# A three-layer graph network on one core: dense tiles and some edge results kept in SBUF between stages, and a row of zeros for each partition

## What is computed

```
h  = relu(layernorm(x))
xn = bn(h, g0, be0)
h  = bn(relu(gcn_conv(xn, src, dst, ew, W1, b1)), g1, be1)                 # 128 -> 256
h  = bn(relu(graph_conv(h, src, dst, ew, Wrel2, brel2, Wroot2)), g2, be2)  # 256 -> 256
h  = bn(relu(graph_conv(h, src, dst, ew, Wrel3, brel3, Wroot3)), g3, be3)  # 256 -> 128
out = x + h

graph_conv(x): agg = segment_sum(ew * x[src], dst);  agg @ Wrel + brel + x @ Wroot
gcn_conv(x):   xw = x @ W; deg = segment_sum(ew, dst) + 1; norm = deg[src]^-.5 * ew * deg[dst]^-.5
               segment_sum(norm * xw[src], dst) + xw / deg + b
bn(x, g, b):   g * (x - mean) * rsqrt(var + eps) + b      (mean and var over the 100,000 nodes)
```

## Time and profile before

| | us |
|---|---|
| median of 3 runs | 3562.28 |
| lowest, highest | 3558.31, 3564.93 |
| profiled execution | 3567.39 |
| its span | 3565.6 |
| TensorE busy | 2930.0 (82%) |
| VectorE busy | 2611.3 (73%) |
| ScalarE busy | 2320.7 (65%) |
| DMA | 1142 MB, 320 GB/s over the span |

### The profile page before, as it was taken

One profiled execution on the slowest core, in us unless ns is written; L12 is line 12 of the kernel. 1 busy time (PEld: TensorE's weight loads), 2 busy tenths in 40 slices (PEclk: granted clock), 3 DMA queues, 4 the chain that ended last, 5 costly groups with the idle time before them and its releaser, 6 DMA issues. The chain is left out here.

```text
span 3565.6 us, 52119 instructions
## 1 busy us (share of the span) xinstructions
PE 2930.0 (82%) x12445; PEld 1951.0 (55%) x12445; DVE 2611.3 (73%) x5600; ACT 2320.7 (65%) x4070; POOL 1332.1 (37%) x1194
## 2 busy tenths in 40 slices
PE   3666599999996799999999999699999999554543
PEld 3665355555553567677777777455555555433432
DVE  6997488888887688888888888568777778433332
ACT  4999377777764677778787778456666666333332
POOL 1657555555551222222222220122223220266476
PEclk9999799999998899999999999899999999555555
DMA  5998499999996899999999999699999999899998
GB/s 200 346 345 301 153 331 333 332 331 333 333 331 240 266 347 341 336 336 341 340 338 342 340 338 313 207 290 344 346 346 351 346 343 321 324 367 364 382 357 238
DMA packets 344636, 1142.09 MB, mean 320 GB/s; under 512 B 55625, under 2 KB 103266, under 8 KB 294386
## 3 DMA queue, kind: packets, MB, share of 16 engines
q1 hardware_dynamic: 221468, 933.98, 69.5%
q0 software_dynamic: 62656, 77.70, 13.5%
q10 hardware_dynamic: 60438, 129.60, 10.2%
HBM read 625.81 MB, written 515.28 MB: 320 GB/s over the span
## 5 line engine op out<-in xcount | busy, mean ns | idle before, releaser
L1210 POOL DMA_INDIRECT l_ed_gathered<-agg_rows,pos_cols x392 | 432.5, 1103 | 1455.0 <-PE l_ps L1222 692.6
L1118 DVE TENSOR_TENSOR l_dn_hi<-l_dn_hi,l_dn_top 128x512 fp32r<-128x512 f32 x784 | 501.1, 688 | 234.5 <-ACT l_dn_top L1086 234.2
L1059 PE MATMUL l_ps<-l_dn_top,wroot_top 128*128 128x512 f32 x1176 | 503.8, 428 | 80.7 <-ACT l_dn_ho L1073 44.2
L1073 ACT ACTIVATE l_dn_ho<-l_ps,bias_fold 128x512 f32<-128x512 f32 x588 | 394.5, 681 | 156.2 <-PE l_ps L1059 155.3
L1086 ACT ACTIVATE l_dn_top<-l_dn_hi 128x512 fp32r<-128x512 f32 x784 | 447.5, 622 | 45.5 <-DMA l_dn_hi<-h_dense 45.5
L1059 PE MATMUL l_ps<-l_dn_hi,wroot_top 128*128 128x512 f32 x1176 | 466.8, 397 | 0.0
L1059 PE MATMUL l_ps<-l_dn_top,wroot_rest 128*128 128x512 f32 x1176 | 466.0, 396 | 0.0
L1648 POOL DMA_INDIRECT out<-out_rows_dst,out_cols x196 | 305.0, 1556 | 282.9 <-DMA out<-out_od_ot 182.7
L716 PE MATMUL l_ps<-l_dn_columns,w_fold 128*128 128x512 f32 x784 | 381.2, 609 | 30.5 <-ACT l_dn_ho L751 30.5
L1107 DVE BATCH_NORM_STATS2 bn_stats_all<-l_dn_ho 128x512 f32 (+1 forms) x588 | 365.7, 679 | 2.4 <-ACT l_dn_ho L1073 2.0
L1669 PE MATMUL out_ps<-ident,out_od_hi 128*128 128x128 f32 x784 | 192.8, 427 | 178.9 <-ACT out_od_hi L1657 178.9
(11 more groups left out here) (237 smaller groups left out, 5797.5 us busy)
## 6 DMA issues: line engine op xcount, KB each, us to landing
h_dense<-l_dn_ho SPq DMA_DIRECT2D x196, 1024.0 KB, 10.8
l_dn_hi<-h_dense SPq DMA_DIRECT2D x196, 1024.0 KB, 10.4
l_dn_rows<-h_rows SPq DMA_DIRECT2D x98, 520.0 KB, 6.4
h_rows<-norm_ln_ho SPq DMA_DIRECT2D x97, 520.0 KB, 4.2
h_dst<-l_ed_ho SPq DMA_DIRECT2D x98, 512.0 KB, 10.3
l_ed_hd<-h_dst ACTq DMA_DIRECT2D x98, 512.0 KB
h_dense<-l_dn_ho SPq DMA_DIRECT2D x98, 512.0 KB, 11.6
out_od_hi<-h_dense SPq DMA_DIRECT2D x98, 512.0 KB, 15.1
```

The source lines that it names most:

```text
L1059: ins = pe.matmul(o, a, b, start=t == 0, stop=t == len(terms) - 1)
L1073: act.activation(ho[:, j, m, c * CW:(c + 1) * CW], ps[:, u % 2, 0:CW], ACT.Relu, bias=bf[:, m:m + 1]).then_inc(rl[j], 1)
L1118: dve.tensor_tensor(rest[:, j, k, cc], hi[:, j, k, cc], top[:, j % 2, k, cc].bitcast(FP), ALU.subtract).then_inc(spl[j], 1)
L1210: pool.indirect_dma_start(tg[:, j, g, :], None, tab[n - 1][:, :], bass.IndirectOffsetOnAxis(ap=pos_c[:, t:t + 1], axis=0)).then_inc(gat[j] ...
```

## The change

It has four parts.

1. The last four dense tiles of l1 are copied from `dn_ho` into a buffer `hi_keep` that lives through l1, l2 and l3, and not stored to DRAM; l2 takes them as its first four tiles. l2 does the same for l3. l3 writes all its results into `ho_keep`, stores all but the last four, and out begins with these. A tile held in a slot keeps it, so the order of the tiles turns by four each time: l1 starts at tile 12 and ends with 8 to 11, so that out has the natural order. The reads of `h0` in l1 follow a list, so l1's last four rounds, not one, are written out (`tail`).
2. In l3 the destination results of even chunks (25 of 49) go to `rows_even` in SBUF, and out reads them there.
3. The first four tiles of x are loaded at the end of l3, where the stores of its last four tiles were.
4. `pos` of a node without incoming edge is EP + p on partition p, so 128 rows of zeros are read and not one. The rows were there already.

```diff
+def order_of(slots, total, moves):
+    order = list(range(total))
+    for _ in range(moves):
+        last = order[:slots]
+        order = order[slots:] + [last[p % slots] for p in range(total - slots, total)]
+    return order
...
+        hi_keep = sb("dense_tiles", [C, NS, 2, W])
...
+                pool.iota(own_zero_row[:, :], pattern=[[0, 1]], base=EP, channel_multiplier=1).then_inc(cst, 1)
...
+                link(dve.tensor_copy(no_edge_row[:, 0, :], own_zero_row[:, :]))
...
-                dve.memset(ho[:, :, :, C:C + 1], float(EP)).then_inc(preset, 1)
+                dve.tensor_copy(ho.rearrange("p s g c -> p (s g) c")[:, :, C:C + 1], no_edge_row.broadcast_to([P, LS * G, 1])).then_inc(preset, 1)
...
+            order = order_of(NS, NT, 3)
             def sync(sp):
                 def load(i, j):
+                    k = i * NS + j
                     wait_use(sp, tu[j], i - 1, CH)
-                    sp.dma_start(ht[:, j, :, :], tile_of(h0, i * NS + j, NP)).then_inc(got[j], 16)
+                    sp.dma_start(ht[:, j, :, :], tile_of(h0, order[k] if isinstance(i, int) else k + 3 * NS, NP)).then_inc(got[j], 16)
                 def store(i, j):
                     wait_use(sp, rl[j], i, per)
-                    sp.dma_start(h1[i * NS + j], ho[:, j, :, :]).then_inc(sto[j], 16)
+                    if isinstance(i, int) and i * NS + j >= NT - NS:
+                        sp.dma_start(hi_keep[:, j, :, :], ho[:, j, :, :]).then_inc(kept[j], 16)
+                    else:
+                        sp.dma_start(h1[i * NS + j], ho[:, j, :, :]).then_inc(sto[j], 16)
...
-            hi = ph.sb("dn_hi", [C, NS, kb, W])
+            hi, kept = hi_keep, ph.slots("dn_kept", NS)
+            def loaded(eng, i, j):
+                if not isinstance(i, int) or i > 0:
+                    wait_use(eng, got[j], i - 1, 16)
             def sync(sp):
                 def load(i, j):
-                    wait_use(sp, mm[j], i - 1, per)
-                    k = i * NS + j
-                    sp.dma_start(hi[:, j, :, :], h_in[k]).then_inc(got[j], 16)
+                    if not isinstance(i, int) or i > 0:
+                        wait_use(sp, mm[j], i - 1, per)
+                        sp.dma_start(hi[:, j, :, :], h_in[(i - 1) * NS + j]).then_inc(got[j], 16)
                 def store(i, j):
-                    wait_use(sp, rl[j], i, per)
-                    sp.dma_start(h_out[i * NS + j], ho[:, j, :, :]).then_inc(sto[j], 16)
+                    if not isinstance(i, int) or i * NS + j < NT - NS:
+                        wait_use(sp, rl[j], i, per)
+                        sp.dma_start(h_out[i * NS + j], ho[:, j, :, :]).then_inc(sto[j], 16)
+                    elif n == 2:
+                        wait_use(sp, rl[j], i, per)
+                        sp.dma_start(hi[:, j, :, :], ho[:, j, :, :]).then_inc(kept[j], 16)
+                    else:
+                        wait_use(sp, mm[j], i, per)
+                        sp.dma_start(x_first[:, j, :, :], tile_of(x, j)).then_inc(kept[j], 16)
                 def end():
                     for j in range(NS):
-                        sp.wait_ge(sto[j], 16 * uses(NS, j))
+                        sp.wait_ge(sto[j], 16 * uses(NS, j, NT - NS))
+                        sp.wait_ge(kept[j], 16)
...
+            def dst_out(i, j, m):
+                if n == 2:
+                    return ho_d[:, j, m, :]
+                return rows_even[:, i, :, :].rearrange("c g w -> c (g w)") if j == 0 else ho_d[:, 0, 0, :]
...
                 def store_dst(i, j):
+                    if n == 3 and j == 0:
+                        return
...
+            held_over = lambda i: dense and isinstance(i, int) and i == 0
             def sync(sp):
                 def load(i, j):
                     k = i * slots + j
+                    if held_over(i) or not dense and j == 0:
+                        return
                     wait_use(sp, tr[j], i - 1, banks)
-                    sp.dma_start(hi[:, j, :], h_in[k].rearrange("c a w -> c (a w)")).then_inc(got[j], 16)
+                    sp.dma_start(hi[:, j, :], h_in[k - dense * slots].rearrange("c a w -> c (a w)")).then_inc(got[j], 16)
...
                 def affine(i, j):
-                    wait_use(act, got[j], i, 16)
-                    act.activation(hi[:, j, :], hi[:, j, :], ACT.Identity, bias=(sft[3] if dense else above_quiet)[:, 0:1], scale=sca[3][:, 0:1]).then_inc(aff[j], 1)
+                    from_sb = not dense and j == 0
+                    if from_sb:
+                        wait_use(act, tr[j], i - 1, banks)
+                    elif not held_over(i):
+                        wait_use(act, got[j], i - dense, 16)
+                    act.activation(hi[:, j, :], rows_even[:, i, :, :].rearrange("c g w -> c (g w)") if from_sb else hi[:, j, :], ACT.Identity,
+                                   bias=(sft[3] if dense else above_quiet)[:, 0:1], scale=sca[3][:, 0:1]).then_inc(aff[j], 1)
...
+        ho_keep = sb("dense_tiles3", [C, NS, 1, W])
+        x_first = sb("x_tiles", [P, NS, G, C])
+        rows_even = sb("rows_dst_even", [P, -(-EC // ES), EG, C])
```

More of the change, by code:

```diff
@@ L146, in pipeline @@
         round_(i)
-    if peeled < rounds - 1:
-        with eng.Fori(peeled, rounds - 1) as i:
+    if peeled < rounds - tail:
+        with eng.Fori(peeled, rounds - tail) as i:
             round_(i)
-    for i in range(max(peeled, rounds - 1), rounds + extra):
+    for i in range(max(peeled, rounds - tail), rounds + extra):
         round_(i)
@@ L156, in uses, with side_by_side @@
     return len(range(j, total or units(slots), slots))
-def side_by_side(ph, rounds, works, total=None, last={}):
+def side_by_side(ph, rounds, works, total=None, last={}, tail=1):
     block = ph.start()
@@ L166, in run @@
         if parts:
-            pipeline(eng, rounds, [(slots, stages, w.get("late", 0)) for w, (slots, stages, _) in parts], total)
+            pipeline(eng, rounds, [(slots, stages, w.get("late", 0)) for w, (slots, stages, _) in parts], total, tail)
             for _, (_, _, end) in parts:
@@ L277, in build, with middle_sb @@
         above_quiet = sb("minus_scaled_quiet3", [C, 1])
-        front = keep.enter_context(ExitStack())
+        hi_keep = sb("dense_tiles", [C, NS, 2, W])
+        middle = keep.enter_context(ExitStack())
+        def middle_sb(name, shape, dt=FP):
+            return middle.enter_context(nc.sbuf_tensor(name, shape, dt))
+        w1, wrel[2] = middle_sb("w1", [C, 1, H1]), middle_sb("wrel2", [C, 2, H1])
+        wparts[2], wrel_parts = [[middle_sb(f"{name}_{part}", [C, 2, H1], FR) for part in ("top", "rest")] for name in ("wroot2", "wrel2")]
+        dst_c, inv_c = middle_sb("dst_cols", [P, ET], I32), middle_sb("inv_deg_src_cols", [P, ET])
+        front = middle.enter_context(ExitStack())
         def front_sb(name, shape, dt=FP):
@@ L1675, in add @@
                 def add(i, j):
-                    if dense:
-                        wait_use(dve, gx[j], i, 16)
+                    if dense and not held_over(i):
+                        wait_use(dve, gx[j], i - 1, 16)
                         wait_use(dve, sto[j], i - 1, 16)
@@ L1681, in add @@
                         part = slice(b * gb, (b + 1) * gb)
-                        rows = ot[:, j, part, :] if dense else rows_dst[:, bass.ds((i * slots + j) * groups, groups), :]
+                        rows = ot[:, j, part, :] if dense else (rows_even, rows_odd)[j][:, i, :, :]
                         turned = ps[0:P, bank0 + (j % 2) * banks + b, 0:gb * C].rearrange("p (g c) -> p g c", g=gb)
@@ L1704, in build @@
             side_by_side(ph, DI, [edges, dense, edges_turn, dense_turn],
[L1705 removed]
+                         last=fold(ph, 1, 2, BN, wroot[2], wfold[2], bias[2], bfold[2], ps), tail=NS)
         front.close()
```

55 lines of the change are left out of this document (29 added, 26 removed).

## The result

The changed kernel takes 3508.9 us (median of 4 runs, 3506.2 to 3512.7), beside 3563.6 (3558.3 to 3565.7) for the kernel before on the same chip: a ratio of 0.9853, 95% interval 0.9838 to 0.9868, 54.7 us less. The forecast was 3514 us and 48 less. The same kernel once more, in a later set of runs: 3508.4, ratio 0.9845 [0.9821, 0.9869].

What follows compares the result with a forecast made beforehand. TensorE was taken to bound the layers, DMA bytes the last stage. Terms 1.8 + 8.6 + 5.1 + 6.6 + 2.6 + 6.8 + 16.9 - 0.3 = 48 us off the 3562.3 us median gave 3514 us; range 3494 to 3542.

Steps and rivals of the forecast that it cites:

- start of l2: cast 1.8, stall 8.6: Layer 2's start: first cast 1.8 us earlier, and TensorE's stall behind VectorE's wait for `ed_coef` 8.6 us shorter.
- steady l2: Layer 2's steady stretch: unchanged, 0 us, since SyncE waits 460 us for TensorE, so loads are late because TensorE is.
- start of l3: cast 5.1, stall 6.6, clock 2.6: Layer 3's start: cast 5.1 us earlier, stall for `ed_same` 6.6 us gone, TensorE's fall to half clock 2.6 us avoided.
- start of the last stage: Start of the last stage: eight loads gone save 10.8 us, less 4.0 us of idle DMA; net 6.8 us.
- even chunks: Last stage: 25 loads of 0.262 MB gone at 387 GB/s, 0.68 us each, 16.9 us saved.
- spreading it frees 768 x 242 ns = 186 engine-us, 11.6 us of all 16: Start of layer 2: gathers no longer reading one zero row take 11.6 us less DMA work, if that row is the reason.
- no stall, no fall: Start of layer 3: without the stall TensorE keeps its clock, 2.6 us saved, of which 0.8 is an estimate.
- the rule weighed in the prediction, 358 GB/s: Last stage: a skill-page HBM-to-SBUF rate, set aside for the measured 370 GB/s; using it would add 2.3 us to the sum.
- C: Rival: DMA is the bound everywhere, so every byte counts; 81 us saved, 3481 us; chance 0.08.
- D: Rival: slow SBUF copies hold up the ends of layers 1 and 2; slower, 3604 us at 20 us a copy; chance 0.04.
- E: Rival: GpSimd's scatters set the last stage's pace, which gains nothing; starts give 10 to 15 us, 3550 us; chance 0.06.
- B: Rival: layer starts keep their stalls, new waits replacing the old; 25 us saved in all, 3537 us; chance 0.22.

Runs made afterwards that it cites:

- last_start_by_dram: The changed kernel, but layer 3's last four tiles go through DRAM and the first four x tiles load at the last stage's start; 3515.1 us, ratio 0.9866.
- even_by_dram: The changed kernel, but layer 3's even chunks are stored to DRAM and loaded again in the last stage; 3522.6 us, ratio 0.9878.
- kept_by_dram: The changed kernel, but the last four tiles of layers 1 and 2 are stored to DRAM and loaded again; 3514.6 us, ratio 0.9860.
- before_again: The kernel before, unchanged, profiled once more; 3568.5 us in one run.
- one_zero_row: The changed kernel with the one zero row of the kernel before put back; 3526.3 us, ratio 0.9886.

## Why the prediction was right, and where it was not

| term | forecast | measured | from |
|---|---|---|---|
| start of l2: cast 1.8, stall 8.6 | 10.4 | 12.4 | `bn_scale` to first of the 75: 209.8, 207.1 before; 196.3, 195.9 after |
| steady l2 | 0 | 4.5 | the 75: 816.1, 814.5; 810.8, 810.7 |
| start of l3: cast 5.1, stall 6.6, clock 2.6 | 14.3 | 16.8 | l3's length; its last 36 mask matmuls take 511.3 us in both |
| start of the last stage | 6.8 | 6.5 | last_start_by_dram |
| even chunks | 16.9 | 14.8 | even_by_dram |
| ends of l1 and l2 | 0 | 0 | kept_by_dram |
| l1 | 0 | 3.0 | not told apart from none |
| setup | -0.3 | none seen | end of norm at 358.5 and 359.1 before, 358.7 and 358.3 after |

**The causes.** The step "spreading it frees 768 x 242 ns = 186 engine-us, 11.6 us of all 16" was right in its mechanism, and in its size: at the start of l2 q0 had 25.0% of 16 x 70 us and has 8.6%, which is 184 engine-us less. It put the rows and the tiles side by side, 11.6 and 10.8 us of DMA work, as if each gave half of the stalls. The runs say otherwise: the rows alone give 26 us of 54.7, the tiles on top of them 3 by the ratios, 6 by the medians and 8 by the stages. Why a us of q0's time weighs more than a us of a tile load isn't shown; that what waits is a small load behind slow packets is only argued. The bounds of 0 to 12.5 us for the stall in l2 held what it gave (12.4 less the cast's 1.8). Of those of 5 to 14.5 us for l3 that can't be said: the first two profiles give 13.5, the means 16.8, and 5 us lie between two executions.

**Why the starts gave more.** The casts moved by 2.3 and 5.0 us, for 1.8 and 5.1. The stalls were sized by the first wait alone, 8.6 and 6.9 us. But VectorE had 11.9 us of such waits at the start of l2 and 19.5 at that of l3 (9.9 and 17.1 in before_again), and both profiles of the change have 1.5 and 4.1 or 4.2. These rows were in the trace of before. In the mean 9.4 and 14.2 us of waits are gone, and besides the casts the starts gave 10.1 and 11.8; which of these waits reach TensorE isn't shown. The term of 2.6 us for the clock, "no stall, no fall", held in part: TensorE was granted 0.66 from 2316 to 2323 and 0.60 from 2323 to 2330 in before, and behind the wait that is left it is granted 0.76 from 2345 to 2350 in one profile of the change and 1.00 in the other.

**The steady part of l2** was forecast at 0, with the argument that SyncE waits 460 us for TensorE. That shows that dense tiles aren't late. It says nothing of ScalarE, whose own DMA issues lasted up to 2.2 us, and who evicts for TensorE. The row that would have told it, the longest issue of `ed_coef` (2181 ns against a median of 783), was there in the trace of before and wasn't read. This step failed, worth 4.5 us; that the long issues are its cause is argued, as said above.

**The last stage** was right to 2 us. The 25 chunks gave 0.59 us each for 0.68 forecast, within its bounds (0.5 to 0.8). The stage's bytes went at 360 GB/s in the row above, not at the same 370; a likely reason, not tested, is that GpSimd's scatters, as many as before, now fall into fewer us. In one window for both, 3060 to 3470, it is 371 before and 366 after, and queue q0's share 19.8% and 22.6%. The Trainium skill, "Perfetto Trace Analysis", Roofline, says that a core on trn2 whose neighbour is idle can draw more than 358 GB/s, up to some 120% of it, and so fits all these rows (103% here), where the rule weighed in the prediction, 358 GB/s, did not.

**The rivals.** C (81 us) is off: with the DMA share down to 0.95, l3's 36 mask matmuls take 511.3 us as they did. Its sign, a shorter steady stretch, did come in l2, but not through the bytes, as said above. Its sum was also too large: the 2.1 MB of x are still loaded, and the bytes moved fell from 1142.1 to 1116.5 MB, 25.6 and not 27.8. D is off, the copies land in 5.0 us. E is off, the last stage followed its bytes. B came true in one_zero_row alone: which stalls come back depended on the fourth part of the change, the zero rows.

**The sum.** The terms measured in the profiles add up to 58 us, the medians differ by 54.7. The two profiled executions of before (3567.4 and 3568.5) lay 4 us above their medians, those of the change (3509.8 and 3507.4) within 1 us of theirs. The executions of one kernel in one set of runs lie 2 to 26 us apart. Against the 48 forecast, the starts and the steady part of l2 were 9 us too small together, l1 3, and the chunks 2 too large.

## What to carry over

If a gather reads one address for all the entries that have nothing to fetch, give it several (eight did here): the one row cost over 200 ns a packet in l2, and 26 us in a kernel whose TensorE was 82% busy. To size a stall at the start of a stage, add up all its waits for the same loads, not the first alone, and look at the longest DMA issue of an engine that also evicts. Add a part alone and undo it alone: the rows gave 26 us in the one and 12 to 17 in the other, and the difference is what other parts remove as well.

## What was not expected of the hardware

- Gathers that read one row of 0.5 KB of DRAM over and over took 306 ns for a packet of 2 KB on average in steady l2; 92 ns with 8 such rows, 86 with 128.
- The issue of a plain DMA by ScalarE took 0.78 to 0.81 us in the median, and at most 2.01 to 2.18, in the three profiles of kernels with the one row and the order and layout of before. With the one row in the changed kernel it was at most 0.91, and with the kept tiles by DRAM as well 1.48.
- On one of the chips all up to the end of norm took 478 and 480 us in the two kernels profiled there, instead of 358, the layers and the last stage about the same as elsewhere.
